# Routed experts on rows gathered by expert group: 19 slots of 512 rows with 8 experts each, in place of 8 chunks of 512 tokens with all 32 experts

## The reference

```python
logits = jnp.einsum('th,eh->te', x, gate_w)            # 4096 tokens, 32 experts
scores = jax.nn.sigmoid(logits); sb = scores + gate_bias
grp = sb.reshape(T, 4, 8)                              # 4 groups of 8 experts
group_scores = jax.lax.top_k(grp, 2)[0].sum(-1)
_, gidx = jax.lax.top_k(group_scores, 2)               # each token keeps 2 of the 4 groups
masked = jnp.where(gmask[:, :, None] > 0, grp, -jnp.inf).reshape(T, 32)
_, topi = jax.lax.top_k(masked, 8)                     # and 8 of the 16 experts left
cw = ...                                               # the chosen scores over their sum, times 2.5
x_lat = x @ fc1_w.T                                    # 256 -> 128
h = relu2(jnp.einsum('tl,eil->eti', x_lat, w1)) * cw.T[:, :, None]
routed = jnp.einsum('eti,eli->tl', h, w2) @ fc2_w.T    # 128 -> 256
shared = relu2(x @ shared_up_w.T) @ shared_down_w.T
```

## Time and profile before

| | |
|---|---|
| median of 3 runs | 3088.99 us |
| the profiled execution | 3089.88 us, its span 3088.1 us |
| busy share of the span | PE 96%, DVE 68%, ACT 60%, POOL 33% |
| first_half | 0 to about 677 us |
| first_attention | about 677 to 1450 us |
| mean granted TensorE clock | 0.988 |

### The profile page before, as it was taken

The page is one execution under the profiler, slowest core; times in us unless marked ns, Lnnn a source line. Parts: engine busy times, 40 slices in busy tenths (PEclk is TensorE's granted clock), DMA queues, the critical chain, the costliest instruction groups (busy, mean ns, idle before and its releaser), DMA issues. The chain is left out here.

```text
span 3088.1 us, 66533 instructions
## 1 busy us (share of the span) xinstructions
PE 2959.2 (96%) x23638; PEld 2227.3 (72%) x23638; DVE 2101.9 (68%) x5890; ACT 1845.5 (60%) x4638; POOL 1016.0 (33%) x1627
## 2 busy tenths in 40 slices
PE   7999999999999999998898999999999999999998
PEld 5888888863344444444787888788887888788886
DVE  5666666679899989994765555655556556565556
ACT  4666666657777777775444555455554556455553
POOL 0000000001100000001005666576665766667663
PEclk9999999989999999999998999999999999999999
DMA  4111111231332323301415545455453554345442
GB/s 153 49 49 49 49 49 42 63 70 32 83 45 58 50 36 66 50 6 38 150 48 133 116 113 117 108 130 119 110 129 94 139 120 112 82 119 128 111 111 73
DMA packets 360644, 262.23 MB, mean 85 GB/s; under 512 B 213116, under 2 KB 295676, under 8 KB 360188
## 3 DMA queue, kind: packets, MB, share of 16 engines
q1 hardware_dynamic: 360316, 257.98, 34.5%
HBM read 100.85 MB, written 44.04 MB: 47 GB/s over the span
## 5 line engine op out<-in xcount | busy, mean ns | idle before, releaser
L1846 ACT ACTIVATE b_pp<-b_pp,b_nm 128x192 f32<-128x192 f32 (+2 forms) x1024 | 473.0, 464 | 472.2 <-DVE b_nm L2024 391.5
L1007 ACT ACTIVATE a_pt<-ps 128x512 f32<-128x512 f32 x1024 | 555.9, 595 | 175.5 <-PE ps L1043 174.5
L176 DVE TENSOR_REDUCE mx<-ps 128x2 f32<-128x1024 f32 x512 | 621.8, 1224 | 55.9 <-PE ps L167 43.4
L1816 POOL TENSOR_SCALAR b_pp<-b_pp,b_rc 128x192 f32<-128x192 f32 x960 | 387.1, 425 | 306.9 <-DVE b_rc L2033 306.9
L797 DVE SCALAR_TENSOR_TENSOR f_yac<-ps,f_cw,f_yac 128x128 f32<-128x128 f32 x992 | 278.0, 343 | 125.4 <-PE ps L596 123.0
L2045 DVE COPY b_pt<-ps 128x320 f32<-128x320 f32 (+2 forms) x336 | 166.2, 508 | 277.8 <-PE ps L1940 262.8
L596 PEld LDWEIGHTS ps<-w,f_sq 128*128 128x128 f32 x2048 | 265.1, 191 | 26.5 <-issue 6.0
L596 PE MATMUL ps<-w,f_sq 128*128 128x128 f32 x2048 | 270.1, 275 | 0.3
L2024 DVE CUSTOM_DVE_ANT_0 b_pp<-ps,b_mk 128x192 f32<-128x192 f32 x480 | 169.8, 354 | 124.7 <-PE ps L1918 124.7
L1975 PE MATMUL ps<-b_wo,b_oT 128*128 128x256 f32 x1024 | 241.6, 380 | 3.7 <-ACT b_vv L1839 3.7
L1056 PE MATMUL ps<-a_pt,a_v 128*32 128x256 f32 x3072 | 241.1, 394 | 0.0
(11 more groups left out here) (291 smaller groups left out, 7752.6 us busy)
## 6 DMA issues: line engine op xcount, KB each, us to landing
b_rt<-b_qf SPq DMA_DIRECT2D x1024, 64.0 KB, 2.0
qk_parts<-f_aa SPq DMA_DIRECT2D x32, 512.0 KB, 2.7
b_vs<-b_vv SPq DMA_DIRECT2D x120, 128.0 KB, 3.0
b_vb<-b_vv SPq DMA_DIRECT2D x120, 128.0 KB, 3.0
b_vs<-b_vv SPq DMA_DIRECT2D x120, 112.0 KB, 2.8
v_rows<-f_va_ SPq DMA_DIRECT2D x16, 512.0 KB, 2.8
rl<-in_W1vT SPq DMA_DIRECT2D x32, 256.0 KB, 3.6
b_wo<-in_W1oT SPq DMA_DIRECT2D x16, 512.0 KB, 3.9
```

What stands on the lines that cost most here:

```text
L176: e.tensor_reduce(M["mx"][kh % 3][:, :, jt, h], P.pair(s), AX.X, ALU.max, negate=True).then_inc(P.free_sem(s), 1)
L1007: e.activation(pt[(4 * i + 2 * j + a) % 12][:, :], P.ap((*s, a)), ACT.Exp).then_inc(P.free_sem((*s, a)), 1)
L1816: m = e.tensor_scalar(x, x, r[:, 2 * u + h:2 * u + h + 1], 1.0, ALU.mult, ALU.mult)
L1846: e.activation(x, x, ACT.Exp, bias=nm[n % 4][:, c:c + 1], scale=-1.0, accum_out=sm[n % 4][:, c:c + 1]).then_inc(exp_done, 1)
```

## The change

The experts no longer run over every token. Each token's latent row (128 values) and the eight weights of a group (ROW = 136 values) are written to a table in memory, latent_rows, once for each of the two groups that it has, at a place found by counting (steps "rank" and "place": the tokens of a group so far, through a product with a triangular matrix of ones; "spot" turns that into row numbers). The table is 16384 rows, first filled with zeros by 16 DMAs from ScalarE's queue ("zero"). POOL writes the rows with indirect DMAs of 128 rows each, 8 per chunk ("scatter"). Then 19 slots run: each is 512 rows of one group, with that group's 8 experts. POOL gathers for each slot four times 128 rows, and the three weight tables w1 high, w1 low and w2 (128 rows of 4 KB each): 7 indirect DMAs, issued when the slot two before has been used up. "xturn" transposes the rows. The number of expert units falls from 8 x 32 = 256 to 19 x 8 = 152. Each slot's result goes to memory, routed_rows ("y_store").

The mixture's second half moves into the first attention. In first_half "part" leaves the shared part alone in g. In the attention, per chunk: "ygather" (8 indirect DMAs on POOL, the two rows of each token), "yadd" (VectorE adds them), "yturn" (four transposes, a copy on ScalarE), and twice "ymix" (products with fc2; VectorE adds the shared part; ScalarE takes Abs, Relu and Exp of 128x512; POOL four operations) and "yrc" (VectorE takes the reciprocal of 128x512, POOL multiplies). This replaces the sigmoid, which is not used in the attention, by Exp, which is. The chunk stage of first_half is now 12 heavy steps, with the steps of the next chunk behind them.

```diff
+G, GE = 4, 8
+NS = 2 * NCH + G - 1
+ROW = 128 + GE
 def first_half_plan():
-        p += [("up", c, 0), ("up", c, 1)]
-        for e in range(E):
...
-            p.append(("down", c, e))
+    heavy = [("qk", 0), ("qk", 1), ("qk", 2), ("qk", 3), ("values", 0), ("values", 1)]
+    heavy += [("shared", j) for j in range(4)] + [("part", 0), ("part", 1)]
+    behind = {0: [("sums",)], 1: [("begin",)], 2: [("turn", 0), ("turn", 1)], 3: [("gate",), ("latent",)],
+              4: [("gate_turn",)], 5: [("groups",)], 6: [("chosen",)], 7: [("eight",)], 8: [("weigh",)],
+              9: [("rank",)], 10: [("place",)], 11: [("spot",), ("scatter",)]}
+        for n, x in enumerate(heavy):
+            p.append((x[0], c, *x[1:]))
...
+            if c + 1 < NCH:
+                p += [(y[0], c + 1, *y[1:]) for y in behind[n]]
+            elif n == 0:
+                p += [("count",), ("slots",)]
+    ups = [(n, e) for n in range(NS) for e in range(GE)]
+    p += [("xturn", 0), ("up", *ups[0]), ("up", *ups[1])]
+    begin = len(ups) - 32
+    for x, (n, e) in enumerate(ups):
+        if e == 3 and n + 1 < NS:
+            p.append(("xturn", n + 1))
...
+        if x + 2 < len(ups):
+            p.append(("up", *ups[x + 2]))
+        if x >= begin and (x - begin) % 2:
+            p.append(("max", (x - begin) // 2))
+        p.append(("down", n, e))
+        if e == GE - 1:
+            p.append(("y_store", n))
+    p += [("both", 0), ("max", 16), ("max", 17), ("rows", 0), ("max", 18)]
 pool:
+                elif k == "scatter":
+                    w.wait_ge(zero_in, 16 * 16)
...
+                    w.wait_ge(spot_set, c + 1)
+                    for i in range(4):
+                        for r in range(2):
+                            e.indirect_dma_start(
+                                X["x_rows"], bass.IndirectOffsetOnAxis(ap=tix[:, 4 * c + i, r:r + 1], axis=0),
+                                rows[(c + 1) % 2][:, i, r, :], None).then_inc(rows_out[c % 2], 16)
+                elif k == "y_store" and c + 2 < NS:
+                    w.wait_ge(*P.filled(("down", c, GE - 1)))
+                    w.wait_ge(*P.emptied(("down", c, GE - 1)))
+                    gather_slot(e, c + 2)
+        def gather_slot(e, n):
+            at, by = slice(n % 2 * GE, n % 2 * GE + GE), wix[:, n:n + 1]
+            for i in range(4):
+                e.indirect_dma_start(xg[n % 2][:, i, :], None, X["x_rows"], bass.IndirectOffsetOnAxis(
+                    ap=xix[:, n, i:i + 1], axis=0)).then_inc(xg_in[n % 2], 16)
+            for x in "hl":
+                e.indirect_dma_start(M[f"w1_{x}"][0][:, at, :].rearrange("p e f -> p (e f)").bitcast(F32), None,
+                                     X[f"w1_{x}"], bass.IndirectOffsetOnAxis(ap=by, axis=0)).then_inc(wg_in[n % 2], 16)
+            e.indirect_dma_start(w2[n % 2][:, :], None, A["w2T"].rearrange("p (g e) f -> (p g) (e f)", g=G),
+                                 bass.IndirectOffsetOnAxis(ap=by, axis=0)).then_inc(wg_in[n % 2], 16)
 scalar:
+                elif k == "zero":
+                    for i in range(16):
+                        e.dma_start(X["x_rows"].rearrange("(a p r) f -> a p (r f)", p=128, r=8)[i],
+                                    rows[0][:, :, :, :].rearrange("p i r f -> p (i r f)")).then_inc(zero_in, 16)
                 elif k == "latent":
+                    if c == 1:
+                        w.wait_ge(zero_in, 16 * 16)
 tensor:
+                elif k == "xturn":
+                    w.wait_ge(xg_in[c % 2], 64 * (c // 2 + 1))
+                    for i in range(4):
+                        m = e.transpose(P.ap(s)[:, i * 128:(i + 1) * 128], xg[c % 2][:, i, 0:128], ident[:, :])
 first_attention_plan:
+    routed = [(s, c, *x) for c in range(NCH) for s, *x in (("yturn",), ("ymix", 0), ("ymix", 1))]
+        if i >= 8 and i % 5 == 3 and routed:
+            x = routed.pop(0)
+            p.append(x)
+            if x[0] == "yturn" and x[1] + 1 < NCH:
+                p.append(("ygather", x[1] + 1))
...
+        m = (i - 10) // 5
+        if i % 5 == 0 and 0 <= m < 3 * NCH and m % 3:
+            p.append(("yrc", m // 3, m % 3 - 1))
 vector, in the attention:
+                elif k == "ymix":
...
+                    e.tensor_tensor(gy, P.ap(s).rearrange("p (i d) -> p i d", d=256), gy, ALU.add).then_inc(P.free_sem(s), 1)
+                elif k == "yrc":
+                    c = s[1]
+                    w.wait_ge(y_pool, 5 * (2 * c + n) + 1)
+                    e.reciprocal(yo[:, :, :], yo[:, :, :]).then_inc(yrc_done, 1)
```

More of the change, by code:

```diff
@@ L321, in first_half @@
                 P.take(s, 4)
-            elif s[0] == "mix_up":
-                if s[3] == 0:
-                    P.take(("mix", *s[1:3]), 2 + s[2])
-            elif s[0] in ("tail_turn", "mix") and s[1] == NCH - 1:
-                if s[0] == "tail_turn":
-                    P.take(s, 5)
-            elif s[0] in ("w_lora", "turn", "gate", "gate_turn", "latent", "qk", "values", "shared", "tail_turn", "mix"):
-                P.take(s, small % 3)
+            elif s[0] == "xturn":
+                P.take(s, 2)
+            elif s[0] in ("w_lora", "turn", "gate", "gate_turn", "latent", "qk", "values", "shared", "part", "place",
+                          "count"):
+                P.take(s, small % 8)
                 small += 1
             elif s[0] == "up":
-                P.take(s, 3 + (s[1] * E + s[2]) % 3)
+                P.take(s, 3 + n_up % 3)
+                n_up += 1
             elif s[0] == "down":
@@ L903, in first_attention @@
                 last = 0
-            elif s[0] in ("rows", "one", "two", "three") or s[:2] == ("weights", "sum"):
+            elif s[0] in ("rows", "one", "two", "three", "yturn", "ymix") or s[:2] == ("weights", "sum"):
                 if last is None:
```

441 lines of the change are left out of this document (312 added, 129 removed).

## The result

The changed kernel takes 3349.58 us (median of 4 runs, 3341.52 to 3355.16) against 3088.01 us of the kernel before on the same chip: ratio 1.0853, 95% interval 1.0835 to 1.0872. It is 8.5% slower. The prediction, 3145 us with a range of 3035 to 3225, had the direction and missed the size: 57 us were forecast, 262 came.

A forecast was written before the change was run, and what follows sets the result against it. TensorE alone was taken to bound first_half, VectorE the first attention. 3088.1 − 32 (first half) + 88.5 (attention) = 3144.6 us span, say 3145; range 3035 to 3225, likeliest case 3095 to 3180.

The forecast's parts named there:

- The chunk period: First half, chunks 1 to 6: 28.6 us of TensorE plus 5.8, 2.3 and 1.2 of waits and clock, 37.9 us each.
- x: Time for which one indirect DMA holds POOL: taken as 1.1 us, between 0.47 and 2.0.
- The issue of the zero fill: Start of first half: 16 DMA issues take 7.5 us of ScalarE; the fill ends at about 64 us.
- The slot's period, 4x + 11.6 = 16.0: First half, slots: waiting for four row gathers sets the period, 16.0 us against TensorE's own 13.2; 18 take 288 us.
- rival D: Slots: weights bind, each slot 2 us later, +36, or +70 with the clock falling; 3181 to 3215 us; chance 0.13.
- The first half, -32: First exponentials at 647 us against 679.2: 32 us gained where 165 us of TensorE work were removed.
- The attention, +88.5: First attention: VectorE's additions 5.5 + 11 + 62 (reciprocals) + 12 + 4 − 6 = +88.5 us.
- ScalarE's additions fit its slack: First attention: 8 copies and 48 operations, 34 us, fit in ScalarE's 16% idle time (53 us), adding nothing.
- Rival A: First half gains far more: indirect DMAs hold POOL only 0.47 us; 3056 us, with further gains 3041 or 3011; chance 0.22.
- Rival B: Indirect DMAs hold POOL 2.0 us: chunks +43, slots +65, late weights +34, about 3285 us; chance 0.10.
- Rival C: The first attention absorbs the reciprocals: 3145 − 62 = 3083 us; chance 0.05.
- The reciprocal's rate: VectorE, 128x512 reciprocal: slopes 6.3, 7.3 and 8 ns a column; 3.9 us taken at 7.3, skill's estimate 4.3.

The follow-up runs named there:

- e4: Changed kernel with three buffers of rows, rows gathered one slot earlier, behind weights that are issued ahead of them: 3208.0 us (kernel before 3088.3).
- e5: The changed kernel run again, unaltered: 3309.0 us (kernel before 3084.5).
- e1: Changed kernel with each of the 16 reciprocals on VectorE replaced by a cheap multiplication of the same tile: 3218.2 us (kernel before 3088.3).
- e3: Changed kernel with the gate by one ScalarE tanh and one POOL instruction, no reciprocal, factor z left out: 3175.4 us (kernel before 3088.3).
- e7: Kernel before with 16 reciprocals of 128x512 on a scratch tile added on VectorE in the first attention: 3179.7 us (kernel before 3084.5).
- e12: Kernel before with the 16 added scratch reciprocals each cut in four of 128x128 over four steps in a row: 3107.3 us (kernel before 3083.8).

## Why the prediction was right and wrong

- **The chunk period: right.** 37.9 us were worked out, 38.6 measured. It is as near as that because two errors offset each other: x was 1.27 in place of 1.1, the wait at "turn" 7.8 in place of 5.8, and the latent products cost less (24 in 2.6 us, where I took 3.8). The last scatter starts at 334.9 us, the chunk stage was to end at 334.
- **The issue of the zero fill: mechanism right, size wrong.** ScalarE was to lose 7.5 us and lost about 18 (14 in 17.57 us, while the DMA engines moved 406 GB/s at a share of 1.02); that the queue takes a DMA only as fast as they empty it is my reading. The sum to 334 held all the same, by luck: from the "turn" of chunk 1 to that of chunk 7 it took 236.5 us in place of 227, and the terms around it were too large by about as much. Which ones I haven't traced.
- **The first slots: 27 us short.** I let the first slot end at 348. POOL starts the gathers of slot 0 at 339.9, its weights' at 345.0, and TensorE starts "up" at 359, after 6.95 us idle. The trace names no releaser there; in e4, where the weights' gathers start 9.5 us later, it names their DMA. Slot 0 ends at about 375.
- **The slot's period, 4x + 11.6 = 16.0: right mechanism, 3.5 us too small.** x gives 0.7 of it, POOL's start behind the last addition 1.3, the low clock behind the wait about 1.3, and two slots lie near 24 us, while the attention's first loads pass through the DMA engines. 18 x 3.5 = 63 us. I had priced the clock behind the wait in the chunks, and for the slots only as a part of rival D, though TensorE's gaps there are nearly as long. The trace puts the wait down to the rows in every slot from the third on, and e4 takes it away.
- **The first half, -32: wrong in sign.** It is +60. 63 and 27 make most of the 92.
- **The attention, +88.5: the step that failed.** It is +204 in the first profile and +162 in e5. The sum priced every added piece by VectorE's time. The reciprocals were sized well (3.34 us; 3.9 put, 53 in place of 62 us), but they cost 95 us in the kernel before, and in the changed one 86 more than a cheap instruction. The other side steps were put at 26.5 and take 35 with the tanh. What I left out is that a lump on VectorE that is longer than TensorE's reserve stops TensorE, and that the attention at the lower clock is bound by TensorE at 4.32 us a step. The earlier trace rows showed the effect, and I used it for first_half only. And the earlier trace rows, from which I took VectorE's 37.5 of 40 us, has TensorE at 38.47 in the same line, by its records: I passed over an engine as full as the one that I named, which left no reserve for a stall or a lower clock. The holes, some 30 to 40 us in the first profile, stood in no term.
- **"ScalarE's additions fit its slack": wrong.** The chain of Abs, Relu, Exp and the operations on POOL costs 45 us beside the tanh (e1 against e3), with 16 us more on ScalarE; up to 12.5 us of it are the cheap instructions on VectorE. The term was put at nothing. How it acts, by lumps of 1.8 us on ScalarE or by banks held, was not tried apart.
- **Rival A** asked for x below 0.7: refuted, POOL's starts lie 1.27 us apart. **Rival B** (x = 2.0) is refuted too, though its 3285 is nearer to the measured time. **Rival C** (the attention absorbs the reciprocals) is refuted by e1 and e7, and e12 shows what it would need. **Rival D** (weights bind): refuted for the period by the waits of the changed kernel, at most 1.34 us between slot 2 and slot 12, against 3.4 to 4.0 for the rows; in the slots while the attention's first loads pass it has a part (1.58 us at 631, and 5.71 in e4).
- **The reciprocal's rate.** The Trainium skill ("VectorE: DVE Perf Modes", "First, the fixed hardware budget") led to an estimate of 4.27 us; the trace says 3.34. The measurement decides: 6.5 ns a column, nearest to the lowest of my three slopes. I wrote that the slope agreed, but the estimate's 8.3 ns a column lay above all three.

## What to carry to other kernels

Work added to the engine that sets the pace has two prices, its sum and its largest piece. Cut it so that each piece fits the slack between two steps: that was worth 72 us in the kernel before, 37 beside the side steps and 30 in the changed kernel, so ask first how much slack is left. Look for a formula of another engine before that (one tanh and two POOL operations replaced a reciprocal, three activations and five POOL operations). And where TensorE is nearly as busy as the engine that sets the pace, work out the stage's time at TensorE's lower clock too: here a step then takes 4.32 us in place of 2.9, and a stall of 3 us was followed by up to 20 us at that clock.
